# Six key tiles multiplied by VectorE straight from PSUM instead of from ScalarE's copies, in a one-core vision-tower kernel

## The chip, the core and the metric

The kernel runs on one NeuronCore of one Trainium2 chip. The metric is the device time of one execution in microseconds (us), the median of several runs. Engines are named as in the profile: PE is TensorE, DVE is VectorE, ACT is ScalarE, POOL is GpSimd, SP is SyncE, which here only issues DMAs.

## What is computed

The reference is a small vision tower on a batch of 64: a patch embedding with window attention and a class token, then a causal attention layer with residual, then a mixture of eight experts with residual. The change touches the window attention of the first stage alone. Cut to that part:

```python
pe   = conv(x, conv_w, stride 14)                   # 6x6 patches of 256 channels
grid = pe.reshape(b, C, 2, 3, 2, 3)                 # 4 windows of 3x3 = 9 positions
red  = grid.mean(axis=(3, 5))                       # one row per window
q    = _ln(red, ...) @ la_wq                        # 8 heads of 32
kv   = _ln(win, ...) @ la_wkv                       # keys and values of the 9 positions
attn = softmax(einsum('bhnd,bhnkd->bhnk', q * C**-0.5, k_), axis=-1)
agg  = einsum('bhnk,bhnkd->bhnd', attn, v_)
local_out = red + agg @ la_proj_w + la_proj_b
```

## The kernel before, in words

The rows of the first stage are (window, batch) pairs: 4 windows times 64 images are 256 rows, two window tiles of 128 partitions. Each window tile has nine positions, so there are 18 position tiles, `i` = 0 to 17; 0 to 8 belong to window tile 0, 9 to 17 to window tile 1 (`wt` in the code). Three position tiles make a group `g`, 0 to 5. The whole program is written out by hand, one instruction stream for each engine, with semaphores.

For each position tile PE makes the convolution (L429, 15 matmuls of 256 columns), ACT copies it to `pe_rows` (L802), DVE takes its mean and variance (L1195 to L1202) and POOL the reciprocal root (L1052). PE turns the group (L453), ACT and DVE split it into a high and a low part (L843, L1315), and PE multiplies it with the joined key and value weights (`keys_values`, L506, six matmuls of 512 columns for one position tile). The 512 columns of a PSUM bank are then 256 columns of keys and 256 of values. Four banks take turns: position tile `i` lands in bank 4 + i % 4. The weights are centred beforehand, so the layer norm's mean needs no subtraction and only its scale `rstd`, one number for each row and position, has to be applied.

`keys_values_copy(g)` (L863) does this on ACT: one instruction for each position tile reads all 512 columns of the bank, multiplies by `rstd` and writes keys and values to `kv_rows`; it then frees the bank (`drained[b]`), and PE may fill it with tile `i + 4`. All keys go to the same place for both window tiles, `keys`, so the copies of window tile 1 wait until the scores of tile 0 have been read (`soft_step`).

`window_scores(wt, k)` on DVE takes three positions at a time: one product of `keys` (128 partitions x 768 elements) with the query row repeated three times (L1235), then a sum over each head's 32 elements into `sc` (L1237). After three of these come the maximum and the difference (L1242, L1244), the exponential on ACT (L883), sum, reciprocal and weights `pn` (L1248 to L1252). DVE and POOL multiply the values by the weights (L355) and add thirds (L360), and PE adds up and turns the result in bank 0 (`tail_agg`, L549), which ACT copies (L874, L875) for the projection (L486). For window tile 0 POOL takes two of the thirds and both sums, and for window tile 1 one of the thirds.

Around the change the order of each engine is this. PE: key/value tiles 12 and 13, the turn of the second query row (`redT1`), tile 14, the query of window tile 1 (`q1`, L486), tiles 15, 16 and 17, `tail_agg(0)`, `tail_proj(0)`, the class token's `qkv_cls` (L626), `tail_agg(1)`. The second half of `tail_agg(1)` waits for DVE's products and its sum (L360). ACT: the two pieces of `redT1` (L806), the copies of tiles 12 to 14, the query copy (L852), a weight rounding (L889), the copies of tiles 15 to 17, the aggregate copy of window tile 0, `window_exp(1)`. DVE: `window_scores(1, 0)`, `(1, 1)`, a small copy of the class token (L1382), `(1, 2)`, `score_maximum(1)`. POOL: the products and sums of window tile 0 (L355, L360), the low part of a weight (L1142, which waits for ACT's L889), the third product of window tile 1.

Of the kernel before, what the change touches and what calls it, by code (L numbers as in the profile page):

```python
# [18 lines left out]
ACT = mybir.ActivationFunctionType  # L19
AX = mybir.AxisListType  # L20
# [6 lines left out]
C = 256  # L27
CC = C // P
NW = 9
TILES = 2 * NW  # L30
GT = 3
GROUPS = TILES // GT
HL, DL = 8, 32
# [18 lines left out]
SOFT = 11  # L52
VSTEPS = 4
REST = KCH[-1][1]
REST_PARTS = ((0, 64), (64, REST))
POOL_FROM = 3
AHEAD_A, AHEAD_B = 3, 2
TOKENS = [(1, 2), (3, 4), (0, 5)]

# [13 lines left out]
def columns(items):  # L73
    at, out = 0, {}
    for name, width in items:
# [18 lines left out]
LNS = ["conv0", "conv1", "class", "conv2", "conv3", "red0", "conv4", "conv5", "red1",  # L94
       "pool0", "pool1", "in0", "in1", "in2", "mid0", "mid1", "mid2"]
# [3 lines left out]
KV_BANKS = 4  # L99
# [19 lines left out]
def tower_kernel(nc, xa, xb, conv_w, tok_w, att_w, consts, biases, rows, ffn_w, out):  # L119
    ctx = ExitStack()  # L120
    with ctx:
        def sb(name, shape, dt=F32):
            return ctx.enter_context(nc.sbuf_tensor(name, shape, dt))

        def sem(name):
            return ctx.enter_context(nc.semaphore(name))
# [19 lines left out]
        rstd = sb("rstd", [P, len(LNS), GT])  # L146
# [3 lines left out]
        kv_rows = sb("kv_rows", [P, 3, NW, C])  # L150
        keys = kv_rows[:, 0, :, :]
        sc = sb("sc", [P, 2, NW, HL])
# [35 lines left out]
        def carve(space, *shapes):  # L188

            at, views = 0, []  # L190
            for shape in shapes:
                n = int(np.prod(shape))
                v, at = space[:, at:at + n], at + n
                names = "abcd"[:len(shape)]
                views.append(v if len(shape) == 1 else v.rearrange(f"p ({' '.join(names)}) -> p {' '.join(names)}", **dict(zip(names, shape))))
            assert at <= space.shape[1]
            return views


        red, redb, rednorm, q_rows, redsum = carve(window[:, :], *[(2, C)] * 5)  # L200
# [25 lines left out]
        inn, hb, acc, midn, ctxT, h = carve(pe_rows[:, :, :, :].rearrange("p w n c -> p (w n c)"),  # L226
                                            (RT, C), (RT, C), (RT, C), (RT, C), (2, T, B), (RT, C))
# [12 lines left out]
        bank = [ctx.enter_context(nc.psum_tensor(f"bank{i}", [P, 512], F32)) for i in range(8)]  # L240
# [28 lines left out]
        drained = [sem(f"drained{i}") for i in range(8)]  # L269
# [15 lines left out]
        rstd_done, normed_done = sem("rstd_done"), sem("normed_done")  # L285
# [6 lines left out]
        third_done = sem("third_done")  # L292
        pool_values, dve_values = sem("pool_values"), sem("dve_values")
        soft_step = sem("soft_step")
        exp_done = sem("exp_done")
        cls_step = sem("cls_step")
        gexp_done, gstep = sem("gexp_done"), sem("gstep")
# [14 lines left out]
        def wait_full(eng, b, name):  # L312

            eng.wait_ge(filled[b], FILLS[b].index(name) + 1)

        def wait_copied(eng, b, name):

            eng.wait_ge(drained[b], FILLS[b].index(name) + 1)

        def wait_split(eng, g):  # L320

            if g == 0:
                eng.wait_ge(x0_split, len(KCH))
            elif g < POOL_FROM:
                eng.wait_ge(x_split, g)
            else:
                eng.wait_ge(x_split_pool, g - POOL_FROM + 1)

# [3 lines left out]
        def spread(ap, axis, n):  # L332

            ap = ap.unsqueeze(axis)
            shape = list(ap.shape)
            shape[axis] = n
            return ap.broadcast_to(shape)
# [82 lines left out]
        def _(pe):  # L420
# [365 lines left out]
            for _, b in OUT_BANKS:  # L786
                pe.wait_ge(drained[b], len(FILLS[b]))
# [6 lines left out]
        def _(act):  # L794
# [50 lines left out]
            def two_pieces(b, name, dst, gain, shift):  # L845
                wait_full(act, b, name)
                affine(dst[:, 0, :], bank[b][:, 0:P], gain, shift, 0)
                affine(dst[:, 1, :], bank[b][:, P:2 * P], gain, shift, 1).then_inc(drained[b], 1)

            def query_copy(wt):  # L850
                wait_full(act, 3, f"q{wt}")
                act.copy(q_rows[:, wt, :], bank[3][:, 0:C]).then_inc(drained[3], 1)  # L852

            def keys_values_copy(g):
                for i in range(GT * g, GT * (g + 1)):
                    wt, n = divmod(i, NW)
                    b = 4 + i % KV_BANKS
                    wait_full(act, b, f"kv{i}")
                    if i >= NW:
                        act.wait_ge(soft_step, 2 * ((i - NW) // GT + 1))  # L860
                    k = LNS.index(f"conv{g}")
                    act.wait_ge(rstd_done, k + 1)
                    act.activation(kv_rows[:, 0:wt + 2:wt + 1, n, :], bank[b][:, :].rearrange("p (k c) -> p k c", k=2),  # L863
                                   ACT.Identity, scale=rstd[:, k, i - GT * g:i - GT * g + 1]).then_inc(drained[b], 1)

# [64 lines left out]
            window_exp(0)  # L930
            turned(5)
            two_pieces(2, "redT1", redT, "q_g", "q_b")
            keys_values_copy(4)
            query_copy(1)
            wait_full(act, CONV_BANK[TILES - 1], f"conv{TILES - 1}")
            weights_hi(0, 0, 16)
            keys_values_copy(5)
# [106 lines left out]
        def _(pool):  # L1044
# [31 lines left out]
            def patches_lo(g):  # L1076
# [5 lines left out]
                                   xs[:, g % 2, HI, 0:n].bitcast(F32), ALU.subtract).then_inc(x_lo_step, 1)  # L1082
                pool.wait_ge(x_lo_step, g - POOL_FROM + 1)
                pool.tensor_tensor(xs[0:rest, g % 2, LO, n:], x_raw[0:rest, g % RAW_X, 4, :],
# [105 lines left out]
        def _(dve):  # L1190
# [36 lines left out]
            def window_scores(wt, k):  # L1227


                ns = slice(GT * k, GT * (k + 1))  # L1230
                step = SOFT * wt + 2 * k
                for i in range(NW * wt + GT * k, NW * wt + GT * (k + 1)):
                    wait_copied(dve, 4 + i % KV_BANKS, f"kv{i}")
                wait_copied(dve, 3, f"q{wt}")
                dve.tensor_tensor(keys[:, ns, :], keys[:, ns, :], spread(q_rows[:, wt, :], 1, GT), ALU.mult).then_inc(soft_step, 1)  # L1235
                dve.wait_ge(soft_step, step + 1)
                dve.tensor_reduce(sc[:, wt, ns, :], keys[:, ns, :].rearrange("p n (h d) -> p n h d", h=HL), AX.X,  # L1237
                                  ALU.add).then_inc(soft_step, 1)

            def score_maximum(wt):  # L1240
                dve.wait_ge(soft_step, SOFT * wt + 6)
                dve.tensor_reduce(smx[:, wt, :], sc[:, wt, :, :].rearrange("p n h -> p h n"), AX.X, ALU.max).then_inc(soft_step, 1)  # L1242
                dve.wait_ge(soft_step, SOFT * wt + 7)
                dve.tensor_tensor(scs[:, wt, :, :], sc[:, wt, :, :], spread(smx[:, wt, :], 1, NW), ALU.subtract).then_inc(soft_step, 1)  # L1244
# [131 lines left out]
            dve.wait_ge(soft_step, SOFT)  # L1376
            value_product(dve, 0, 2).then_inc(third_done, 1)
            window_scores(1, 0)
            window_scores(1, 1)

            wait_full(dve, 3, "q1")
            dve.tensor_copy(hT[:, :, 0, :, :].rearrange("p c s b -> p c (s b)"), spread(tokT[:, :], 2, P)).then_inc(tok_cols, 1)  # L1382
            window_scores(1, 2)
            score_maximum(1)


# [275 lines left out]
```

## Time and profile before

| | |
|---|---|
| median of 3 runs | 234.22 us (233.64 to 235.34) |
| profiled execution | 234.87 us, its span 233.1 us |
| PE busy | 205.5 us (88% of the span) |
| DVE busy | 158.8 us (68%) |
| ACT busy | 101.4 us (44%) |
| POOL busy | 95.6 us (41%) |
| chain that ended last | PE 64%, DVE 13%, issue 9%, POOL 4%, ACT 4% |
| mean granted TensorE clock | 0.971 |

The span runs from the first to the last instruction in the trace; 1.8 us of the execution's time lie outside it. The first 130 us are the two attention stages, the rest the experts, in which PE is busy almost throughout. The chain that ended last is followed back from the last instruction, at each step to what released it. In the first stage it changes from engine to engine every few microseconds, and the places that matter for the change lie between 76 and 97 us. The granted clock is the share of TensorE's full 2.4 GHz: 1.00 is that level, 0.50 is 1.2 GHz, and a value between them is a stretch in which it changed.

### The profile page before, as it was taken

The numbers are of one execution on the slowest core, as the hardware profiler recorded it, in microseconds if no ns is written. First come the engines' busy times: TensorE is split into PE (matmuls) and PEld (weight loads), VectorE is DVE, ScalarE is ACT, GpSimd is POOL, SyncE is SP. The second block draws the span as 40 slices with busy tenths as digits, with TensorE's granted clock in tenths as the row PEclk, the third lists the DMA queues.
The fourth block names the chain that finished last, engine by engine and source line by source line (L and its number), as shares of the span: only waits on it lengthen the run. The fifth ranks groups of instructions, "written<-read, shape, count | busy, mean of one in ns | idle before, by whom it ended". The sixth has DMA issues, their size and how long they took to land.

```text
span 233.1 us, 3936 instructions
## 1 busy us (share of the span) xinstructions
PE 205.5 (88%) x1332; PEld 190.2 (82%) x1332; DVE 158.8 (68%) x357; ACT 101.4 (44%) x225; POOL 95.6 (41%) x100
## 2 busy tenths in 40 slices
PE   2989958999998973869588899999999999999984
PEld 2988938998996853747476799999999999999983
DVE  2567791586448799577987589577676776767641
ACT  3863660635334724234231157365636463626120
POOL 0054399695143963246464305333232333333200
PEclk9999997999999998899999859999999999999999
DMA  6999900008500000000000003460706071500004
GB/s 232 385 400 366 307 4 0 6 0 325 218 0 0 1 0 3 0 0 0 1 3 0 0 0 87 187 245 30 270 17 253 0 270 38 232 0 0 3 0 68
DMA packets 4890, 23.01 MB, mean 99 GB/s; under 512 B 694, under 2 KB 2444, under 8 KB 3724
## 3 DMA queue, kind: packets, MB, share of 16 engines
q1 hardware_dynamic: 3960, 21.26, 25.1%
q10 hardware_dynamic: 916, 1.58, 2.0%
q8 instruction: 8, 0.13, 0.2%
q14 instruction: 6, 0.05, 0.1%
HBM read 22.44 MB, written 0.39 MB: 98 GB/s over the span
## 4 chain that ended last, share of the span: by engine, by line
PE 64%; DVE 13%; issue 9%; POOL 4%; ACT 4%; DMA 2%; SPq 2%; ACTq 0%; DVEq 0%; POOLq 0%
PE bank L752 26%; PE bank L765 14%; PE bank L429 9%; PE bank L506 4%; PE bank L642 2%; DVE kv_rows L1235 2%; DMA raw<-xb 2%; POOL rstd L1052 2%; PE bank L549 2%; DVE stats L1195 2%; PE bank L651 1%; POOL window L1066 1%; SPq L350 1%; PE bank L453 1%; PE bank L672 1%
## 5 line engine op out<-in xcount | busy, mean ns | idle before, releaser
L752 PE MATMUL bank<-split 128*128 128x322 f32 x384 | 60.8, 320 | 0.0
L752 PEld LDWEIGHTS bank<-split 128*128 128x128 f32 x384 | 59.5, 195 | 0.0
L1180 POOL TENSOR_TENSOR split<-raw,split 128x256 fp32r<-128x256 f32 x32 | 29.0, 908 | 58.6 <-DVE split L1517 58.6
L765 PE MATMUL bank<-split 128*128 128x256 f32 x288 | 36.1, 283 | 0.6 <-DVE split L1570 0.6
L765 PEld LDWEIGHTS bank<-split 128*128 128x128 f32 x288 | 35.4, 192 | 0.8 <-DVE split L1570 0.8
L429 PE MATMUL bank<-split 128*128 128x256 f32 (+1 forms) x225 | 29.9, 294 | 0.7 <-DVE split L1294 0.7
L429 PEld LDWEIGHTS bank<-split 128*128 128x128 f32 (+1 forms) x225 | 28.8, 201 | 0.8 <-DVE split L1294 0.8
L506 PE MATMUL bank<-split 128*128 128x512 f32 x108 | 26.5, 397 | 0.0
L1019 ACT ACTIVATE vprod<-bank 128x322 f32<-128x322 f32 x32 | 14.0, 436 | 25.4 <-PE bank L752 25.3
L1564 DVE TENSOR_TENSOR vprod<-bank,vprod 128x322 f32<-128x322 f32 x32 | 15.8, 493 | 13.3 <-PE bank L752 9.3
L506 PEld LDWEIGHTS bank<-split 128*128 128x128 f32 x108 | 19.8, 188 | 3.9
L1052 POOL TENSOR_TENSOR rstd<-veps,mhalf 128x1 f32<-128x1 f32 (+2 forms) x17 | 11.4, 670 | 27.2 <-DVE veps L1202 27.0
L1027 ACT CAST split<-vprod 128x322 fp32r<-128x322 f32 x32 | 14.8, 463 | 16.7 <-DVE vprod L1564 16.6
L1512 DVE TENSOR_TENSOR split<-raw,split 128x512 fp32r<-128x512 f32 x29 | 20.1, 692 | 2.2 <-ACT split L889 2.1
L889 ACT CAST split<-raw 128x512 fp32r<-128x512 f32 x32 | 19.5, 613 | 2.4 <-DMA raw<-ffn_w 2.4
L1195 DVE BATCH_NORM_STATS2 stats<-pe_rows 128x6 f32<-128x256 f32 x24 | 9.0, 415 | 15.2 <-ACT pe_rows L802 15.0
L1556 DVE SCALAR_TENSOR_TENSOR pe_rows<-bank,wgt,pe_rows 128x256 f32<-128x256 f32 x24 | 11.2, 479 | 11.1 <-PE bank L765 11.1
L802 ACT COPY pe_rows<-bank 128x256 f32<-128x256 f32 x18 | 6.5, 374 | 24.7 <-PE bank L429 23.8
L1570 DVE TENSOR_TENSOR split<-vprod,split 128x322 fp32r<-128x322 f32 x32 | 15.9, 498 | 1.4 <-ACT split L1027 1.4
L1066 POOL TENSOR_TENSOR window<-window,pe_rows 128x256 f32<-128x256 f32 x14 | 11.7, 836 | 11.3 <-ACT pe_rows L802 10.5
L863 ACT ACTIVATE kv_rows<-bank,rstd 128x512 f32<-128x512 f32 x18 | 12.0, 690 | 6.8 <-PE bank L506 6.7
L444 PE MATMUL bank<-split 128*128 128x256 f32 (+1 forms) x45 | 7.8, 342 | 4.7 <-ACT split L816 4.7
(165 smaller groups left out, 290.9 us busy)
## 6 DMA issues: line engine op xcount, KB each, us to landing
raw<-ffn_w SPq DMA_DIRECT2D x8, 1536.0 KB, 6.5
raw<-xa SPq DMA_DIRECT2D x5, 768.0 KB
tok<-tok_w SPq DMA_DIRECT2D x1, 1536.0 KB, 11.8
tok<-tok_w SPq DMA_DIRECT2D x1, 776.0 KB, 5.9
raw<-xa ACTq DMA_DIRECT2D x1, 576.0 KB, 4.4
raw<-xb SPq DMA_DIRECT2D x6, 96.0 KB
att<-att_w SPq DMA_DIRECT2D x1, 488.0 KB, 13.2
raw<-conv_w SPq DMA_DIRECT2D x1, 384.0 KB, 5.3
```

The lines of the kernel that those rows point to most:

```text
L429: mm = pe.matmul(bank[b][:, 0:C], xs[0:n, g % 2, px, a:a + P], cws[0:n, pw, k, :], start=(k == 0 and m == 0), stop=(k == len(KCH) - 1 and ...
L506: mm = pe.matmul(bank[b][:, :], lns[:, g % 2, px, a:a + P], wkvs[:, pw, aw:aw + 2 * C], start=(c == 0 and m == 0), stop=(c == CC - 1 and m ...
L752: mm = pe.matmul(bank[b][:, 0:NCOL], aws[:, q, pw, a:a + P], ms[:, px, c, FIRST:ROWS], start=(c == 0 and m == 0), stop=(c == CC - 1 and m ...
L765: mm = pe.matmul(bank[b][:, 0:C], hids[:, px, s * FQ + q, a:a + P], bws[:, s, pw, q * C:(q + 1) * C], start=(q == 0 and m == 0), stop=(q = ...
L889: act.copy(aws[:, q, HI, :], a_raw[:, slot, q, :]).then_inc(a_hi, 1)
L1027: act.copy(hids[:, HI, s * FQ + q, FIRST:ROWS], hidf[:, q % 2, :]).then_inc(hid_hi, 1)
L1052: pool.tensor_tensor(rstd[0:parts, k, 0:n], veps[0:parts, k, 0:n], mhalf[0:parts, 0:n], ALU.pow).then_inc(rstd_done, 1)
L1066: pool.tensor_tensor(redsum[:, wt, :], pe_rows[:, wt, 0, :] if n == 1 else redsum[:, wt, :], pe_rows[:, wt, n, :], ALU.add).then_inc(sum_s ...
L1180: pool.tensor_tensor(bws[:, s, LO, q * C:(q + 1) * C], b_raw[:, s, q, :], bws[:, s, HI, q * C:(q + 1) * C].bitcast(F32), ALU.subtract).the ...
L1512: dve.tensor_tensor(aws[:, q, LO, :], a_raw[:, slot, q, :], aws[:, q, HI, :].bitcast(F32), ALU.subtract).then_inc(a_split, 1)
L1564: dve.tensor_tensor(hidf[:, q % 2, :], bank[5 + q % 2][:, 0:NCOL], sg[:, q % 2, :], ALU.mult).then_inc(hid_done, 1)
L1570: dve.tensor_tensor(hids[:, LO, s * FQ + q, FIRST:ROWS], hidf[:, q % 2, :], hids[:, HI, s * FQ + q, FIRST:ROWS].bitcast(F32), ALU.subtract ...
```

## The change

For the last six position tiles (groups 4 and 5, `i` = 12 to 17) DVE no longer reads keys that ACT has copied. `direct_scores(k)` takes the place of `window_scores(1, 1)` and `(1, 2)`: for each position one product of the bank's first 256 columns, in PSUM, with the query row; then the same sum over heads; then a new small product of the 24 sums with `rstd`, since the keys are not scaled any more. ACT copies and scales only the 256 value columns of these tiles, and waits for `keys_read`, which DVE raises after its product of the same tile. The bank is freed by ACT's copy as before. The query copy on ACT moves ahead of the copies of group 4.

```diff
+DIRECT = 4
...
+                    if g >= DIRECT:
+                        act.wait_ge(keys_read, i - GT * DIRECT + 1)
+                        act.activation(kv_rows[:, 1 + wt, n, :], bank[b][:, C:2 * C], ACT.Identity,
+                                       scale=rstd[:, k, i - GT * g:i - GT * g + 1]).then_inc(drained[b], 1)
+                        continue
...
+            query_copy(1)
             keys_values_copy(4)
-            query_copy(1)
...
+            def direct_scores(k):
+
+                g, wt = NW // GT + k, 1
+                ns = slice(GT * k, GT * (k + 1))
+                step = SOFT * wt + 2 * k
+                wait_copied(dve, 3, f"q{wt}")
+                for i in range(GT * g, GT * (g + 1)):
+                    b = 4 + i % KV_BANKS
+                    wait_full(dve, b, f"kv{i}")
+                    n = GT * k + i - GT * g
+                    ins = dve.tensor_tensor(keys[:, n, :], bank[b][:, 0:C], q_rows[:, wt, :], ALU.mult).then_inc(keys_read, 1)
+                dve.wait_ge(keys_read, GT * (g - DIRECT + 1))
+                dve.tensor_reduce(sc[:, wt, ns, :], keys[:, ns, :].rearrange("p n (h d) -> p n h d", h=HL), AX.X,
+                                  ALU.add).then_inc(soft_step, 1)
+                dve.wait_ge(soft_step, step + 1)
+                dve.wait_ge(rstd_done, LNS.index(f"conv{g}") + 1)
+                dve.tensor_tensor(sc[:, wt, ns, :], sc[:, wt, ns, :], spread(rstd[:, LNS.index(f"conv{g}"), :], 2, HL),
+                                  ALU.mult).then_inc(soft_step, 1)
...
-            window_scores(1, 1)
+            direct_scores(1)
...
-            window_scores(1, 2)
+            direct_scores(2)
             score_maximum(1)
```

On ACT, between the pieces of `redT1` and the exponential of window tile 1, the order before is this (`window` is the query row here, `filled4` means bank 4 is full, `keys_read` counts DVE's products):

```order
L806 ACTIVATE redT<-bank,tok 128x128
L863 ACTIVATE kv_rows<-bank,rstd 128x2x256 [waits rstd_done,soft_step,filled4]
L863 ACTIVATE kv_rows<-bank,rstd 128x2x256 [waits rstd_done,soft_step,filled5]
L863 ACTIVATE kv_rows<-bank,rstd 128x2x256 [waits rstd_done,soft_step,filled6]
L852 COPY window<-bank 128x256 [waits filled3]
L889 CAST split<-raw 128x512 [waits ffn_in0,filled0]
L863 ACTIVATE kv_rows<-bank,rstd 128x2x256 [waits rstd_done,soft_step,filled7]
```

and in the changed kernel (whose line numbers are a few higher):

```order
L808 ACTIVATE redT<-bank,tok 128x128
L854 COPY window<-bank 128x256 [waits filled3]
L867 ACTIVATE kv_rows<-bank,rstd 128x256 [waits rstd_done,keys_read,soft_step,filled4]
L867 ACTIVATE kv_rows<-bank,rstd 128x256 [waits rstd_done,keys_read,soft_step,filled5]
L867 ACTIVATE kv_rows<-bank,rstd 128x256 [waits rstd_done,keys_read,soft_step,filled6]
L896 CAST split<-raw 128x512 [waits ffn_in0,filled0]
L867 ACTIVATE kv_rows<-bank,rstd 128x256 [waits rstd_done,keys_read,soft_step,filled7]
```

The query copy has gone ahead of the three copies, each copy is half as wide, and each waits for `keys_read`.

On DVE, from the scores of the first third of window tile 1 to the maximum, before (`vprod` and `kv_rows` are values, keys and their products):

```order
L1235 TENSOR_TENSOR kv_rows<-kv_rows,window 128x768 [waits drained7,drained3,drained6,drained5]
L1237 TENSOR_REDUCE sc<-kv_rows 128x24 [waits soft_step]
L1235 TENSOR_TENSOR kv_rows<-kv_rows,window 128x768 [waits drained6,drained3,drained5,drained4]
L1237 TENSOR_REDUCE sc<-kv_rows 128x24 [waits soft_step]
L1382 COPY tok<-tokT 128x2x128 [waits filled3]
L1235 TENSOR_TENSOR kv_rows<-kv_rows,window 128x768 [waits drained5,drained3,drained4,drained7]
L1237 TENSOR_REDUCE sc<-kv_rows 128x24 [waits soft_step]
L1242 TENSOR_REDUCE smx<-sc 128x8 [waits soft_step]
```

and in the changed kernel, behind the first third's product, which stands as before:

```order
L1244 TENSOR_REDUCE sc<-kv_rows 128x24 [waits soft_step]
L1257 TENSOR_TENSOR kv_rows<-bank,window 128x256 [waits filled4,drained3]
L1257 TENSOR_TENSOR kv_rows<-bank,window 128x256 [waits filled5]
L1257 TENSOR_TENSOR kv_rows<-bank,window 128x256 [waits filled6]
L1259 TENSOR_REDUCE sc<-kv_rows 128x24 [waits keys_read]
L1263 TENSOR_TENSOR sc<-sc,rstd 128x24 [waits rstd_done,soft_step]
L1408 COPY tok<-tokT 128x2x128 [waits filled3]
L1257 TENSOR_TENSOR kv_rows<-bank,window 128x256 [waits filled7,drained3]
L1257 TENSOR_TENSOR kv_rows<-bank,window 128x256 [waits filled4]
L1257 TENSOR_TENSOR kv_rows<-bank,window 128x256 [waits filled5]
L1259 TENSOR_REDUCE sc<-kv_rows 128x24 [waits keys_read]
L1263 TENSOR_TENSOR sc<-sc,rstd 128x24 [waits rstd_done,soft_step]
```

Each product of 768 elements has become three of 256 that wait for a bank to be full (`filled`) and not for ACT's copy (`drained`), and each sum has a small product with `rstd` behind it. The order on PE and on POOL is the same in both kernels.

## Rows read from the trace of the kernel before

**Rows 1.** Chain that ended last, 78 to 92 us: start us, us, what
```profile
78.46 0.41 ACT window L852
...
78.99 2.47 DVE kv_rows L1235
...
82.36 1.61 DVE kv_rows L1235
...
87.12 0.29 DVE smx L1242
...
88.93 2.26 POOL vprod L355
...
91.32 4.42 PE bank L549 x24
```

**Rows 2.** Timeline, 75 to 93 us: start us, us, engine, line, operation, out<-in
```profile
75.07 3.64 POOL L355 TENSOR_TENSOR vprod<-kv_rows,pn 128x768 f32<-128x768 f32 x2 [0.93 <-DVE pn L1252]
...
77.91 4.48 PE L506 MATMUL bank<-split 128*128 128x512 f32 x18
...
78.78 4.35 POOL L360 TENSOR_TENSOR vprod<-vprod 128x768 f32<-128x768 f32 x2
...
79.69 0.69 ACT L863 ACTIVATE kv_rows<-bank,rstd 128x512 f32<-128x512 f32 x1 [0.31 <-PE bank L506]
...
82.43 0.69 ACT L863 ACTIVATE kv_rows<-bank,rstd 128x512 f32<-128x512 f32 x1 [0.67 <-PE bank L506]
...
83.28 1.58 PE L549 MATMUL bank<-con,vprod 128*128 128x128 f32 x12 [0.90 <-POOL vprod L360]
...
85.58 1.13 PE L486 MATMUL bank<-tok,aggT 128*128 128x256 f32 x4 [0.72 <-ACT aggT L875]
...
86.54 0.92 PE L626 MATMUL bank<-att,tok 128*128 128x224 f32 x4
...
92.03 0.96 DVE L360 TENSOR_TENSOR vprod<-vprod 128x768 f32<-128x768 f32 x1
```

**Rows 3.** Sources: durations in ns (minimum, median, maximum), first and last start
```profile
L1266 DVE TENSOR_TENSOR lo<-bank,window x2: 415/420/425, 92.9 to 97.6; 128x256 f32<-128x256 f32 x2
L1315 DVE TENSOR_TENSOR split<-bank,split x12: 540/548/551, 24.6 to 75.4; 128x384 fp32r<-128x384 f32 x12
L802 ACT COPY pe_rows<-bank x18: 361/373/390, 12.6 to 66.5; 128x256 f32<-128x256 f32 x18
L1361 DVE TENSOR_TENSOR gqblk<-con,gqc x1: 1552/1552/1552, 51.1 to 51.1; 128x16 f32<-128x16 f32 x1
```

**Rows 4.** Timeline of DVE, 67 to 72 us: three 256-column operations, a 768-column sum
```profile
67.05 1.08 DVE L1195 BATCH_NORM_STATS2 stats<-pe_rows 128x6 f32<-128x256 f32 x3 [5.83 <-ACT pe_rows L802]
...
70.50 0.95 DVE L1237 TENSOR_REDUCE sc<-kv_rows 128x24 f32<-128x768 f32 x1
```

**Rows 5.** Waits of PE: us in total, times, longest us
```profile
PE bank L549 <- POOL vprod L355: 3.9, 1, 3.9
PE bank L515 <- DVE split L1315: 3.5, 1, 3.5
```

**Rows 6.** Windows of one us: busy time and count by engine, granted clock, DMA share
```profile
36.00:37.00 1.00, 1.00 (x7) 1.00 (x8) 0.32 (x3) 0.00 (x0) 0.83 (x3) 0.71 0.00 0
...
91.00:92.00 1.00, 0.68 (x3) 0.71 (x4) 0.99 (x1) 0.00 (x0) 0.18 (x1) 0.52 0.00 0
...
94.00:95.00 1.00, 1.00 (x9) 1.00 (x8) 0.29 (x2) 0.00 (x0) 0.73 (x2) 0.78 0.00 0
...
132.00:133.00 1.00, 1.00 (x5) 0.74 (x4) 0.42 (x1) 0.37 (x1) 0.03 (x1) 0.50 0.00 0
...
138.00:139.00 1.00, 1.00 (x6) 1.00 (x5) 0.90 (x4) 0.09 (x1) 0.00 (x0) 0.59 0.00 0
```

**Rows 7.** Timeline of PE: 45 convolution matmuls at the full clock, and with a slow stretch
```profile
14.01 5.66 PE L429 MATMUL bank<-split 128*128 128x256 f32 x45 [0.71 <-DVE split L1294]
...
35.85 7.11 PE L429 MATMUL bank<-split 128*128 128x256 f32 x45
```

More of the change, by code:

```diff
@@ L294, in tower_kernel @@
         soft_step = sem("soft_step")
+        keys_read = sem("keys_read")
         exp_done = sem("exp_done")
```

## The prediction

> **What bounds the kernel now.** I read the page for the shares first: PE is busy most of the span, but the expert stages make up most of that. So the second view is the chain that ended last, cut to the place of the change [rows 1]. There the reader is to see that PE does not lead: the query copy on ACT (78.46) releases DVE, whose three products and sums follow one another up to the maximum at 87.12, then come the weights, POOL's product from 88.93, and PE's `tail_agg(1)` from 91.32. The first product takes 2.47 us and the second 1.61, the same work as elsewhere 0.95, because POOL's two sums run beside them from 78.78 for 4.35 us [rows 1, 2].
>
> The third view is the timeline of PE and ACT [rows 2]. The 18 matmuls of tiles 15 to 17 run without a break, 77.91 to 82.39. ACT takes tile 15 at 79.69 and tile 17 at 82.43, so two tiles take 2.74 us of PE, 1.37 each, and a reader follows its tile's last issue by 0.4 us (77.91 + 3 x 1.37 = 82.02, read at 82.43). Tile 16 needs bank 4, in which tile 12 stood. ACT had emptied it long before. This is what the change touches.
>
> The fourth view is the granted clock [rows 5, 6]. PE sat idle twice for over 3 us: 3.5 us before L515 and 3.9 us before `tail_agg(1)`. Behind each the clock fell to half: the us from 36 shows 0.71 on its way down, the us from 91 shows 0.52, and it was back in the us from 94 (0.78). One such stretch cost 45 convolution matmuls 7.11 - 5.66 = 1.45 us [rows 7].
>
> **The change part by part.** All in us of the profiled execution.
>
> Query copy first on ACT. It began at 78.46, when the last of the three wide copies was ending; PE's query matmuls were ready hardly earlier. I count 0, at most 0.1 gained. The first third's product and sum on DVE stand as before, so the next DVE product starts at 82.36 as now.
>
> The second third. One product of 1.61 goes, three of 256 columns from PSUM come. The nearest row is L1266, 0.42 each [rows 3]; three 256-column operations in a row take 1.08 in all [rows 4]. Does POOL hold them up as it did the wide product? L1315 also reads one operand from PSUM and one from SBUF, and its twelve runs stay between 540 and 551 ns, the last pair of them beside POOL's products from 75.07 [rows 2, 3]. So I take 1.08: ends at 83.44, against 83.97 before. Bounds: 1.61 if POOL holds them up after all, 1.08 if not. The sum is unchanged, 0.95 [rows 4], and the rescaling is added: its nearest row is the maximum over 72 elements, 0.29 [rows 1], taken as 0.25. Everything before the class token's copy is then 0.1 to 0.3 earlier than now, and worth nothing, since the next wait ends later.
>
> One bound of the rescaling is bad: it has two SBUF operands, and L1361, 16 elements wide, took 1.55 us where POOL was at work [rows 3]. Here the rescaling starts near 84.5, and POOL's L1142 near 84.6, since ACT's rounding now stands behind the new copies. If POOL comes first, DVE loses up to 1.3 us, and 0 to 0.7 of that reaches the last product below.
>
> The new wait, on ACT. The copy of tile 12 now needs DVE's product of tile 12: 82.36 + 0.42 = 82.78. Behind it on ACT queue the copies of tiles 13 and 14, the rounding, and the copies of tiles 15 to 17; behind its release of bank 4 waits PE with tile 16, and behind that in PE's order stand tile 17, `tail_agg(0)`, the projection and `qkv_cls`. A 256-column copy out of PSUM took 0.37 [rows 3], the 512-column one 0.69 [rows 2]; I take 0.42. Bank 4 is free at 83.25 and PE starts tile 16 at 83.3, where before it started at 77.91 + 1.37 = 79.3. PE is idle from 79.3 plus the end of its pipeline, some 3.7 to 4 us.
>
> The last product. At the full clock tile 17 can be read at 83.3 + 2 x 1.37 + 0.4 = 86.45. Then product 0.42, step 0.05, sum 0.95, step 0.05, rescaling 0.25, step 0.05: the maximum starts at 88.2, against 87.12. That is +1.1. The products of tiles 15 and 16 lie beside PE's work and cost nothing.
>
> The clock in this new hole. An idle time of 3.5 us and one of 3.9 us both brought it down [rows 5, 6]; the new one lies between the two. A low stretch that begins as PE resumes takes 1.45 from tiles 16 and 17 [rows 7]: the maximum starts at 89.7, +2.55.
>
> What is given back behind it. The chain from the maximum to the end of DVE's sum (L360, 92.03 + 0.96 = 92.99 [rows 2]) moves along unchanged. But the old hole in PE closes: `tail_agg(0)`, projection and `qkv_cls` (1.58, 1.13 and 0.92 [rows 2], with ACT's copy between them) now follow tile 17 and reach to within 2 us of `tail_agg(1)`. So I expect no low clock there. Its 24 records took 4.42; at the full clock 12 of them take 1.58 [rows 1, 2], and the second twelve start when DVE's sum is done. With +2.55: sum at 95.54, then 0.05 and 1.58, end at 97.17, against 91.32 + 4.42 = 95.74. Net +1.4. ACT's aggregate copy, which stands ahead of the exponential, is ready about when the exponential is, and is hidden.
>
> **Sum.** 0 for the query copy, +2.55 at the maximum, -1.15 at `tail_agg(1)`: +1.4, so 234.87 + 1.4 = 236.3 for an execution like the profiled one. That one lies 0.65 above the median of the runs, 234.22, so on the median I forecast 235.6. This kernel's measurement can tell about 1% (2.3 us) from no change.
>
> The Trainium skill (TensorE: Matmul & The Clock Gate, Part 1) says that the chip's watching of PE's activity is free-running and does not reset when a kernel starts. The trace agrees as far as it goes: the clock fell some 3.6 to 4 us behind the start of each idle time, not at one fixed distance. By that rule a low stretch can fall partly beside the two tiles, and the cost of 1.45 is then its upper end.
>
> **The rivals.**
>
> First, the clock stays full across the new hole. Then only +1.1 arrives at the maximum, DVE's sum ends at 94.09, and `tail_agg(1)` at 94.09 + 0.05 + 1.58 = 95.7, as now: 0.0, so 234.2 on the median. For it: the hole ends with dense matmuls. Against it: both idle times of this length brought the clock down. 25%.
>
> Second, slower by over 1%: the clock stays low twice as long. This is what the trace shows around 132 to 139 (0.50 and then 0.59 on its way up [rows 6]). There PE had short and mixed matmuls behind a gap, as it has here in `tail_agg(0)`, projection and query. Then all 2.74 of tiles 16 and 17 runs slow. At the convolutions' rate (1.45 lost in about 3.4 of slow clock) that is +2.0, the maximum +3.1, and if the clock is low again in `tail_agg(1)`, its second half takes 2.7: 96.1 + 2.7 = 98.8, +3.1 in all, 237.3 on the median. It decides once the low clock outlasts tile 17. 12%.
>
> Third, faster: PE's two low stretches near 132 are short by one, because the work arrives there at another moment. One stretch is 1.45, so with the first rival it gives 232.7. Nothing in the profile ties it to the change. 5%.
>
> That the change doesn't unhook DVE from ACT is no rival: the order shows the products waiting for `filled` alone.
>
> **How the numbers follow.** Forecast 58%, first rival 25%, second 12%, third 5%. The range goes from 233.8, a little under the first rival, to 237.4, just above the second; it leaves out the third. Slower by over 1% means above 236.6: the second rival and a few per cent of the forecast's own spread, where the rescaling is held up too: 0.15. Faster by over 1%, below 231.9: 0.05. Within 1%: 0.80.
>
> **What would show it.** In the profile after: DVE's products from PSUM at 0.42 each, the first near 82.4; the first narrow copy of ACT at 82.8; PE idle before tile 16 from about 79.7 to 83.3, released by ACT's copy; a granted clock of 0.5 in the us from 84 to 86; the maximum near 89.7; the clock at 1.0 in `tail_agg(1)`, its end near 97.2. The forecast is wrong if the clock is full at 84, if the products take over 0.6, or if PE starts tile 16 before 82.

## The result, and the profile after

The changed kernel takes 238.05 us (237.18 to 238.06, 4 runs) against 234.36 us before (233.64 to 235.34, 4 runs): ratio 1.0139, 95% interval 1.0102 to 1.0177. Two later comparisons of the same pair gave 1.0155 (1.0100 to 1.0210) and 1.0121 (1.0075 to 1.0167). Over all 16 runs of the changed kernel the median is 237.46 us, over the 87 runs of the kernel before that list a clock 234.44: 3.0 us slower, where 1.4 were forecast. The profiled execution took 238.05 us, its span 236.3. The ratios leave out the runs more than 1.5% above a kernel's fastest, and since those are the ones with the most slow clock, every count of slow stretches below, and every mean time, is over all runs instead.

The place of the change in the timeline of the changed kernel (start us, us, engine, line, operation), which answers to [rows 1, 2]:

```profile
80.28 0.37 ACT L854 COPY window<-bank 128x256 f32<-128x256 f32 x1 [1.44 <-PE bank L488]
...
80.78 2.62 DVE L1242 TENSOR_TENSOR kv_rows<-kv_rows,window 128x768 f32<-128x768 f32 x1 [1.43 <-ACT window L854]
...
84.30 1.07 DVE L1257 TENSOR_TENSOR kv_rows<-bank,window 128x256 f32<-128x256 f32 x3
84.83 1.20 ACT L867 ACTIVATE kv_rows<-bank,rstd 128x256 f32<-128x256 f32 x3 [4.18 <-DVE kv_rows L1257]
...
85.45 4.35 PE L508 MATMUL bank<-split 128*128 128x512 f32 x12 [3.82 <-ACT kv_rows L867]
...
86.40 0.18 DVE L1263 TENSOR_TENSOR sc<-sc,rstd 128x24 f32<-128x24 f32 x1
...
86.62 1.31 POOL L1149 TENSOR_TENSOR split<-raw,split 128x512 fp32r<-128x512 f32 x1 [1.56 <-ACT split L896]
...
89.84 0.42 DVE L1257 TENSOR_TENSOR kv_rows<-bank,window 128x256 f32<-128x256 f32 x1 [2.14 <-PE bank L508]
...
90.38 0.47 ACT L867 ACTIVATE kv_rows<-bank,rstd 128x256 f32<-128x256 f32 x1 [2.09 <-DVE kv_rows L1257]
...
91.51 0.28 DVE L1268 TENSOR_REDUCE smx<-sc 128x8 f32<-128x72 f32 x1
...
95.72 3.32 PE L551 MATMUL bank<-con,vprod 128*128 128x128 f32 x24 [1.74 <-POOL vprod L357]
```

The reader is to see the new chain: DVE's first direct product (84.30) releases ACT's narrow copy (84.83), that releases PE (85.45), whose 12 matmuls of tiles 16 and 17 take 4.35 us, and only then comes DVE's last product (89.84). The maximum starts 11.23 us after the query copy (91.51 - 80.28), where it was 87.12 - 78.46 = 8.66 [rows 1]. `tail_agg(1)` takes 3.32 in place of 4.42.

The longest waits of PE in it, beside [rows 5]:

```profile
PE bank L508 <- ACT kv_rows L867: 3.8, 1, 3.8
PE bank L517 <- DVE split L1341: 3.5, 1, 3.5
...
PE bank L551 <- POOL vprod L357: 1.7, 1, 1.7
```

The hole of 3.9 us before `tail_agg(1)` has shrunk to 1.7, and one of 3.8 has opened before tile 16.

The granted clock in windows of one us (the number before the last two), beside [rows 6]:

```profile
35.00:36.00 1.00, 0.00 (x0) 0.00 (x0) 0.96 (x6) 0.00 (x0) 0.86 (x2) 0.77 0.00 0
42.00:43.00 1.00, 1.00 (x9) 1.00 (x9) 0.00 (x0) 0.00 (x0) 0.92 (x2) 0.81 0.00 0
87.00:88.00 1.00, 1.00 (x4) 0.77 (x3) 0.54 (x2) 0.65 (x2) 0.93 (x1) 0.50 0.00 0
107.00:108.00 1.00, 0.81 (x2) 0.81 (x3) 0.64 (x3) 0.09 (x1) 0.76 (x2) 0.61 0.00 0
121.00:122.00 1.00, 0.55 (x3) 0.51 (x3) 0.93 (x3) 0.39 (x2) 1.00 (x3) 0.50 0.00 0
```

The clock is at half from 35.6 to 42.4, 86.8 to 90.2, 107.2 to 110.6 and 120.9 to 124.3. Before, it was so from 36.4 to 39.8, 91.0 to 94.5 and 132.0 to 138.8. The us that were spent at half clock are 17.1 here and 13.7 before, always in portions of 3.4 or twice that. I call 3.4 us at half clock a slow stretch: five here, four before.

That gave a second way to read every run, not only the profiled one. Each run lists its span and its mean granted clock, and 2 x (1 - clock) x span is the time at half clock. A line through these 103 runs of the two kernels, with one slope and two offsets, leaves a scatter of 0.5 us (standard deviation; the farthest run lies 1.4 us off): 231.1 us for the kernel before and 232.7 for the changed one, plus 0.33 us for each us at half clock, 1.1 for a stretch. The kernel before has a mean of 3.1 stretches a run (2, 3 or 4), the changed kernel 4.4 (3, 4 or 5). So the 3.0 us are two things: 1.6 that are there at an equal number of stretches, and 1.3 stretches more (plus or minus 0.4), 1.4 us. At the same number of stretches, which the forecast had assumed, the medians are 234.4 and 236.35 at three, and 235.6 and 236.7 at four: 1.9 and 1.1 apart.

### The profile page after: what moved, and what is told of

Read it like the earlier page. It is cut to its first block, busy times and chain, and to the rows that moved or that the text cites. A ratio compares the mean times of both kernels' runs of the same rounds, so it can differ in the third digit from the quotient of the medians.

```text
span 236.3 us, 3948 instructions
## 1 busy us (share of the span) xinstructions
PE 207.5 (88%) x1332; PEld 191.7 (81%) x1332; DVE 159.2 (67%) x363; ACT 100.5 (43%) x225; POOL 94.0 (40%) x100
## 4 chain that ended last, share of the span: by engine, by line
PE 66%; DVE 13%; issue 8%; ACT 4%; POOL 3%; DMA 2%; SPq 2%; ACTq 0%; DVEq 0%; POOLq 0%
PE bank L754 25%; PE bank L767 14%; PE bank L431 9%; PE bank L508 6%; DMA raw<-xb 2%; PE bank L644 2%; PE bank L628 2%; POOL rstd L1059 2%; DVE stats L1202 1%; PE bank L455 1%; PE bank L653 1%; DVE vprod L357 1%; PE bank L488 1%; POOL window L1073 1%; SPq L352 1%
## 5 line engine op out<-in xcount | busy, mean ns | idle before, releaser
L754 PE MATMUL bank<-split 128*128 128x322 f32 x384 | 59.2, 314 | 0.6 <-DVE vprod L1590 0.6
L508 PE MATMUL bank<-split 128*128 128x512 f32 x108 | 28.1, 413 | 3.8 <-ACT kv_rows L867 3.8
L431 PE MATMUL bank<-split 128*128 128x256 f32 (+1 forms) x225 | 30.8, 300 | 0.2 <-DVE split L1320 0.2
L431 PEld LDWEIGHTS bank<-split 128*128 128x128 f32 (+1 forms) x225 | 29.7, 207 | 0.3 <-DVE split L1320 0.3
L508 PEld LDWEIGHTS bank<-split 128*128 128x128 f32 x108 | 20.6, 196 | 8.3 <-issue 4.2
L1538 DVE TENSOR_TENSOR split<-raw,split 128x512 fp32r<-128x512 f32 x29 | 20.6, 712 | 2.2 <-ACT split L896 2.2
L446 PE MATMUL bank<-split 128*128 128x256 f32 (+1 forms) x45 | 8.6, 368 | 5.4 <-ACT split L818 5.4
L446 PEld LDWEIGHTS bank<-split 128*128 128x128 f32 (+1 forms) x45 | 8.1, 273 | 5.7 <-ACT split L818 5.7
```

The costliest lines, as they stand in the source:

```text
L431: mm = pe.matmul(bank[b][:, 0:C], xs[0:n, g % 2, px, a:a + P], cws[0:n, pw, k, :], start=(k == 0 and m == 0), stop=(k == len(KCH) - 1 and ...
L446: mm = pe.matmul(bank[j][:, 0:C], xs[0:n, 0, px, a:a + P], cws[0:n, pw, k, :], start=(k == 0 and m == 0), stop=(k == len(KCH) - 1 and m == 2))
L508: mm = pe.matmul(bank[b][:, :], lns[:, g % 2, px, a:a + P], wkvs[:, pw, aw:aw + 2 * C], start=(c == 0 and m == 0), stop=(c == CC - 1 and m ...
L754: mm = pe.matmul(bank[b][:, 0:NCOL], aws[:, q, pw, a:a + P], ms[:, px, c, FIRST:ROWS], start=(c == 0 and m == 0), stop=(c == CC - 1 and m ...
L1538: dve.tensor_tensor(aws[:, q, LO, :], a_raw[:, slot, q, :], aws[:, q, HI, :].bitcast(F32), ALU.subtract).then_inc(a_split, 1)
```

## The experiments

All counts of stretches below are made in this way. "At equal clock" means the offset of such a line, one slope (1.1 us a stretch) for all kernels; differences between kernels are known to about 0.5 us. This table has, for each profiled execution, the start of the second query copy on ACT, the time from it to the maximum (the part that the change touches), and from there to DVE's second `local_out` (L1266 before, L1292 in the changed kernel), which holds `tail_agg(1)`:

| kernel | query copy at | to the maximum | on to `local_out(1)` |
|---|---|---|---|
| before | 78.46 | 8.66 | 10.49 |
| before again (e1) | 79.69 | 8.67 | 10.63 |
| changed | 80.28 | 11.23 | 9.41 |
| changed again (e2) | 79.53 | 11.43 | 9.41 |
| changed, third (e8) | 78.69 | 12.23 | 10.64 |
| last group only (e3) | 81.52 | 9.14 | 10.69 |
| products early (e4) | 81.06 | 8.53 | 10.80 |
| hole filled (e5) | 79.49 | 9.89 | 10.73 |
| before, filled (e6) | 79.85 | 8.66 | 9.42 |
| early and filled (e7) | 76.91 | 8.55 | 9.42 |
| before, late tile 16 (e9) | 80.07 | 12.89 | 9.41 |
| both filled (e10) | 79.73 | 9.90 | 9.41 |
| products early, again (e11) | 80.69 | 8.56 | 10.76 |

### e1: the kernel before again, no edit

> The kernel before, unchanged, run once more as if it were a change. Of the 3.2 us between the two profiled executions, 1.9 to 2.0 us stand in the traces before the place of the change is reached (at the query copy, 78.46 against 80.28): about 0.96 from the first input transfer and about 1.0 from a slow TensorE stretch behind the wait at L515 that lasted 6.8 us and not 3.4. Theory A (this part is variation from run to run, and no effect of the change): the ratio is 1.000 within 0.5%, single times are spread over 1 to 2 us, and its profile may show another number or length of slow stretches, with a span of 231 to 236. Theory B (this part belongs to the changed program): the stretch behind L515 lasts 3.4 us again and the first transfer takes 4.7 us, as in the first profile.

Measured: ratio 1.0014 (0.9972 to 1.0055), single runs 233.25 to 236.67 us. Its profile reaches the query copy at 79.69, 1.2 us later than the first profile of the very same kernel, with slow clock for 6.8 us behind L515, where the first profile had 3.4. So what lies ahead of the change's place in the first pair of profiles is variation from run to run: theory A. The changed kernel itself reaches the query copy at 79.53 and 78.69 in e2 and e8.

### e2 and e8: the changed kernel again, no edit

> The changed kernel, unchanged, once more. Theory A: 1.2 to 2 us slower than before in the median (the +1.4 at the place of the change and little else), and the stretch behind L515 can be short in its profile. Theory B: 3 to 4 us slower again, with the long stretch behind L515 and the slow transfer back in the profile, and two slow stretches near 107 and 121 us. Both expect the hole of 3.8 us in front of tile 16 and a slow stretch behind it.

> The changed kernel once more beside the others on one chip, to count its slow stretches. Clock theory: a mean of 4 to 5 a run again, base 233.4, 237.5 to 238.3 in the median. If the count of 4.5 was chance: near 3, median 236.3 to 236.8. Its profile gives a third picture of where the stretches lie; a place that comes back each time (near 107 and near 120 us) would be an effect of the change, a place that does not is chance.

Measured: 1.0155 and 1.0121. The early slow stretch was short in both profiles, so on that point theory A held, but its 1.2 to 2 us did not: the loss stayed. Neither 107 nor 120 came back in all three (e2 has a stretch at 119 to 122.5, e8 neither), so nothing ties those places to the change. What came back each time is the hole before tile 16 and slow clock behind it. The counts are 4.5 and 4.2 stretches a run. e8's count is in the range that was expected, but its median of 236.72 is not: it lies with the other case, 236.3 to 236.8. In e8 both tiles 16 and 17 and `tail_agg(1)` were slow, as in the prediction's second rival. Its PE timeline:

```profile
83.85 5.37 PE L508 MATMUL bank<-split 128*128 128x512 f32 x12 [3.81 <-ACT kv_rows L867]
...
95.13 4.54 PE L551 MATMUL bank<-con,vprod 128*128 128x128 f32 x24 [1.97 <-POOL vprod L357]
```

and its clock:

```profile
84.00:85.00 1.00, 1.00 (x3) 0.81 (x4) 0.97 (x3) 0.94 (x3) 0.00 (x0) 0.50 0.00 0
88.00:89.00 1.00, 1.00 (x4) 0.81 (x3) 0.00 (x0) 0.00 (x0) 0.00 (x0) 0.51 0.00 0
```

Tiles 16 and 17 ran almost wholly at half clock (5.37 us for 12 matmuls, against 4.35 in the first profile and 3.0 in e5), and `tail_agg(1)` was slow again behind an idle time of only 1.97 us. From the query copy to `local_out(1)` that is 22.9 us, 3.7 more than before. The length of that idle time does not decide it: in e2 `tail_agg(1)` ran at the full clock behind the same 1.97 us:

```profile
95.16 3.32 PE L551 MATMUL bank<-con,vprod 128*128 128x128 f32 x24 [1.97 <-POOL vprod L357]
```

### e3: direct products for the last group only

```diff
-DIRECT = 4
+DIRECT = 5
...
-            direct_scores(1)
+            window_scores(1, 1)
```

> Direct products for the last three position tiles only (DIRECT = 5, window_scores(1, 1) restored). The banks of tiles 12 to 14 are then freed by ACT at once and PE has no hole in front of tile 16. If the late release of the banks is the cause: within 0.5 us of the kernel before (DVE pays three products of 1.07 for one of 0.95 and 0.2 for the rescaling: +0.3 to +0.4), no wait of PE before tile 16, the slow stretch in tail_agg(1) back. If the direct products as such cost the time (slower products, contention): about half of the loss stays, +1 us or more.

Measured: 1.0009 (0.9964 to 1.0054); over all 12 runs the mean is 0.35% above that of the kernel before (interval -0.1% to +0.8%), with 4.1 stretches a run against 2.9. No wait of PE before tile 16. DVE behind the second group:

```profile
88.34 1.07 DVE L1257 TENSOR_TENSOR kv_rows<-bank,window 128x256 f32<-128x256 f32 x3
89.45 0.95 DVE L1259 TENSOR_REDUCE sc<-kv_rows 128x24 f32<-128x768 f32 x1
90.44 0.18 DVE L1263 TENSOR_TENSOR sc<-sc,rstd 128x24 f32<-128x24 f32 x1
```

Three products take 1.07 and the rescaling 0.18 and a step, so the maximum comes 0.48 later than before, of which 0.35 is these two. The direct products as such cost that and no more: at equal clock this kernel is not above the one before (0.3 us below). For the 1.6 us it is the release of tiles 12 to 14 that matters, since only their banks have a successor that PE is about to fill. On the number of stretches this run leaves a doubt: it has no hole before tile 16, and 1.2 stretches more than the kernel before (plus or minus 1.0), two of them in its profile's `tail_agg(1)`, behind a wait of only 1.54 us:

```profile
94.87 4.60 PE L551 MATMUL bank<-con,vprod 128*128 128x128 f32 x24 [1.54 <-POOL vprod L357]
```

e4 and e11 below, with all six products direct and no hole either, have no more stretches than the kernel before.

### e4 and e11: all six direct, but the first three ahead of the wide product

`direct_scores` is cut in two, and DVE's three products of tiles 12 to 14 go first:

```diff
+            direct_products(1)
             window_scores(1, 0)
             direct_scores(1)
...
+            direct_products(2)
             direct_scores(2)
```

> The changed kernel with DVE's three direct products of tiles 12 to 14 moved ahead of window_scores(1, 0), so that ACT can free their banks before PE needs them; all else as in the changed kernel. Late-release theory: PE's wait before tile 16 falls from 3.8 us to under 0.3, the slow stretch there goes, the maximum starts within 0.6 us of the kernel before, and the time is within 0.7 us of the kernel before, 2 to 3 us under the changed kernel. Rival (the direct products or the rescaling cost it): it stays within 1 us of the changed kernel.

> The version with the early direct products, once more, since its first interval (0.982 to 0.997) was wide. From the query copy to the maximum it took 8.5 us against 8.7 before, so at equal clocks I expect no more than 0.3 us of gain: ratio 0.997 to 1.001. If the 0.9895 holds, it comes from fewer slow stretches (mean under 2.7 a run against 3.1).

Measured: 0.9895 (0.9819 to 0.9972) and 0.9949 (0.9916 to 0.9983). Over all 6 and all 12 runs the means are 0.45% and 0.38% below that of the kernel before (intervals -1.3% to +0.4%, and -0.7% to 0.0%), so the version is a little faster at best, and about 4 us under the changed kernel, more than the 2 to 3 expected. e11's ratio is below the 0.997 to 1.001 that was expected. The timeline of e4 shows why the loss is gone:

```profile
81.46 1.09 DVE L1255 TENSOR_TENSOR kv_rows<-bank,window 128x256 f32<-128x256 f32 x3 [1.35 <-ACT window L854]
...
82.46 1.71 DVE L1242 TENSOR_TENSOR kv_rows<-kv_rows,window 128x768 f32<-128x768 f32 x1
...
82.62 3.00 PE L508 MATMUL bank<-split 128*128 128x512 f32 x12 [0.21 <-ACT kv_rows L867]
...
86.06 1.09 DVE L1267 TENSOR_TENSOR sc<-sc,rstd 128x24 f32<-128x24 f32 x1
```

PE waits 0.21 us and not 3.8. The wide product, started later beside POOL's sums, takes 1.71 and not 2.5 to 2.6. The rescaling is the bad case of the prediction's bound: 1.09 us for 24 elements, because POOL's L1149 began at 85.84. The 8.53 us to the maximum are hardly less than 8.66; at equal clock this kernel lies 0.8 us under the one of before, and I can name only 0.1 of that from the traces. The rest is open. It does not come from fewer stretches, as e11's expectation had it: over all 18 runs there are 3.0 a run, as many as before.

### e5: the hole before tile 16 filled with spare matmuls

```diff
+            keys_values(GT * 5)
+            pe.wait_ge(att_in, 16)
+            for _ in range(6):
+                pe.matmul(bank[2][:, 0:C], ident, att[:, 0:C], start=True, stop=True)
+            keys_values(GT * 5 + 1)
+            keys_values(GT * 5 + 2)
-            keys_values_group(5)
```

> The changed kernel with six spare matmuls of 256 columns (about 0.5 us each, 3 us in all) on PE between tile 15 and tile 16, into a free bank: PE is busy in most of the hole, and starts tile 16 when it did before. Each run lists its mean granted clock, from which 2 x (1 - clock) x span gives the us spent at half clock; over the runs so far the time is a base of the kernel (231.7 before, 233.4 changed) plus 0.97 us for each stretch of 3.4 us at half clock, with 3.1 such stretches a run before and 4.5 changed. Clock theory (the hole brings slow stretches of its own): one to two stretches a run fewer, tiles 16 and 17 at the full clock, 1.0 to 1.9 us faster than the changed kernel. Rival (the number of slow stretches has to do with something else, such as the later stages): tiles 16 and 17 at the full clock, but the count stays above 4 and the time within 0.7 us of the changed kernel.

Measured: 1.0004 (0.9970 to 1.0039), 2.5 stretches a run. (The added wait lets the spare matmuls start only when their operand is loaded; each shows as two records in the trace.) The release of tile 16 is exactly as late as in the changed kernel; only the clock differs:

```profile
80.68 2.75 PE L616 MATMUL bank<-att,con 128*128 128x256 f32 x12
84.67 3.01 PE L508 MATMUL bank<-split 128*128 128x512 f32 x12 [1.23 <-ACT kv_rows L872]
```

Tiles 16 and 17 take 3.01 and not 4.35 or 5.37. The maximum comes 9.89 us after the query copy, 1.23 later than before, and that is what the late release costs by itself at this place. What the maximum came later still in the changed kernel (11.23, 11.43 and 12.23) was clock. Nothing was gained in this one profile behind it: `tail_agg(1)` was slow there, and `local_out(1)` comes 20.6 us after the query copy, as in the first profile of the changed kernel. The gain stands in the runs: 1.9 stretches fewer than in the changed kernel (1.7 fewer than in e8 on the same chip), at the upper end of the expected one to two, and a mean 2.0 us below e8's, where 1.0 to 1.9 were expected. At equal clock the two kernels are 0.4 us apart, which is within the error.

### e6 and e7: the old hole filled

Six spare matmuls between `qkv_cls` and `tail_agg(1)`, in the kernel before (e6) and in the version of e4 (e7):

```diff
             qkv("qkv_cls")
+            for _ in range(6):
+                pe.matmul(bank[2][:, 0:C], ident, att[:, 0:C], start=True, stop=True)
             tail_agg(1, (*range(2 * GT, NW), *range(GT)))
```

> The kernel before with the same six spare matmuls in its own hole of 3.9 us, between qkv_cls and tail_agg(1). Clock theory: tail_agg(1) takes 3.2 to 3.4 us and not 4.4, one slow stretch a run fewer (about 2), 0.9 to 1.3 us faster than before. Rival: the slow stretches only fall elsewhere, no faster than before by 0.3 us. This is also the price of what I took to be given back at tail_agg(1) by the change.

> The version with the early direct products and the six spare matmuls before tail_agg(1). If both gains add: base as e4 (230.7) and one slow stretch a run fewer, 232 to 233 in the median, 1.5 to 2 us faster than before. If they do not: at e4's time.

Measured: e6 0.9938 (0.9898 to 0.9978). Over all 12 runs the mean is 0.3% below that of the kernel before (interval -0.7% to +0.05%), with 2.3 stretches a run against 3.0 on the same chip (0.6 fewer, plus or minus 0.7). So a gain is likely, but smaller than the 0.9 to 1.3 us expected, and not shown beyond the noise. In the profile `tail_agg(1)` takes 3.32 us and starts 4.2 us after the maximum as before:

```profile
88.69 2.75 PE L681 MATMUL bank<-att,con 128*128 128x256 f32 x12
92.72 3.32 PE L549 MATMUL bank<-con,vprod 128*128 128x128 f32 x24 [1.28 <-POOL vprod L355]
```

e7 1.0015 (0.9984 to 1.0046): the median is 234.47, not the 232 to 233 of two gains that add, and over all 13 runs the mean equals that of the kernel before (234.2 against 234.3), with 2.9 stretches a run. The profiled run is the fastest of them (230.15 us, with no slow stretch in its span), 8.55 and 9.42 us in the two parts. Filling this place gave nothing here.

### e9: the kernel before with tile 16 started late

```diff
+            keys_values(GT * 5)
+            pe.wait_ge(soft_step, SOFT + 3)
+            keys_values(GT * 5 + 1)
+            keys_values(GT * 5 + 2)
-            keys_values_group(5)
```

> The kernel before with one wait added: PE starts tile 16 only when DVE's second wide product is done, some 5.5 us behind the query copy, about when the changed kernel does (5.2). No direct product, no rescaling, no other order. Late-start theory (the hole in PE is the whole cause): from the query copy to the maximum 11.4 us at the full clock and up to 12.8 with a slow stretch (8.7 before, 11.2 to 12.2 changed), 4 to 5 slow stretches a run, 2.5 to 4 us slower than before. Rival (the direct products, the narrow copies or the rescaling have a good part in it): at most 1.5 us slower than before.

Measured: 1.0167 (1.0088 to 1.0246), and 236.99 to 241.82 us over its six runs with 3 to 7 stretches, 5.4 in the mean against 3.2 before on the same chip. Over all six the mean is 2.3% above that of the kernel before (1.5% to 3.2%), 5.5 us, more than the 2.5 to 4 expected. PE waits 4.3 us:

```profile
PE bank L506 <- DVE kv_rows L1238: 4.3, 1, 4.3
```

12.89 us to the maximum, with a slow stretch on tiles 16 and 17, for which up to 12.8 was expected. Nothing of the change is in this kernel but the late start of tile 16, and it loses as much and more: 3.2 us at equal clock, and 2.2 stretches. More, because its third product has to wait for ACT's wide copy of tile 17 as well. Here `tail_agg(1)` ran at the full clock behind an idle time of 3.17 us:

```profile
97.17 3.32 PE L549 MATMUL bank<-con,vprod 128*128 128x128 f32 x24 [3.17 <-POOL vprod L355]
```

### e10: the changed kernel with both places filled

As e5, and three spare matmuls before `tail_agg(1)`:

```diff
             qkv("qkv_cls")
+            for _ in range(3):
+                pe.matmul(bank[2][:, 0:C], ident, att[:, 0:C], start=True, stop=True)
```

> The changed kernel with PE kept busy in both places: six spare matmuls before tile 16 and three more before tail_agg(1). If the count of slow stretches is made by these two places: about 2 a run (2.5 with the first place alone, 4.4 in the changed kernel), 234.3 to 235.0 in the median, with tail_agg(1) at 3.2 to 3.4 us. If not: at e5's 235.3.

Measured: 0.9988 (0.9947 to 1.0030), median 234.54 and 2.1 stretches a run, both as expected. `tail_agg(1)` at 3.32 us:

```profile
91.70 1.46 PE L688 MATMUL bank<-att,con 128*128 128x256 f32 x6
93.84 3.32 PE L551 MATMUL bank<-con,vprod 128*128 128x128 f32 x24 [0.68 <-POOL vprod L357]
```

Filling the second place took 0.4 of a stretch more off than e5 did, which is within the noise. That place is slow in some profiles (e8, e5) and not in others (the first one, e2), while the first was slow in all three profiles of the changed kernel.

## Why the prediction was wrong, point by point

- **Query copy first: 0.** Right. It starts right behind PE now, but DVE's first product starts 0.5 us after it, as before. Nothing is gained.
- **The products from PSUM, 0.42 each, 1.08 for three, not held up by POOL.** Right: 416 ns in the median of six, 412 to 425, and 1.07 for three; the first of them ran beside POOL's sum, the fourth (86.70) beside POOL's L1149. The rescaling took 0.18 in all three profiles of the changed kernel, not 0.25; it went ahead of POOL's L1149 by 0.2 us. The bad bound was real and shows in e4 (1.09).
- **The new wait.** Right: PE idle 3.8 us; ACT's narrow copy 0.47, not 0.42.
- **The late release by itself: +1.1 at the maximum.** 1.23 in e5. Over the runs the change costs 1.6 at equal clock.
- **One slow stretch on tiles 16 and 17: +2.55 in all.** +2.57 in the first profile and +2.77 in e2, but +3.57 in e8, where the clock was low for 6.8 us and so through both tiles. That also answers the sentence that took 1.45 for the upper end. The reading beside it was a little off: in the trace before, the clock fell 4.2 and 3.6 us behind the start of the two idle times. In the changed kernel it fell 5.1 us behind it, at 86.75 and not at 84, in e2 4.0 and in e8 2.1.
- **Given back at `tail_agg(1)`: -1.15.** -1.08 in the first profile and e2, which makes +1.5 and +1.7 from the query copy to `local_out(1)`, as forecast. In e8 nothing was given back, and it is +3.7.
- **The comparison of two executions.** Of the 3.2 us between the two first profiles, 1.8 lie ahead of the query copy (78.46 against 80.28), and e1 shows 1.2 of variation there in the kernel before alone. Of the first four runs of the changed kernel three had five stretches. So a part of the distance between 238.05 and the range was the draw; the median of all 16 runs, 237.46, lies at its upper end.

The step that failed is the count of slow stretches in "What is given back behind it". The sum set one stretch on tiles 16 and 17 against one taken off `tail_agg(1)` ("So I expect no low clock there") and so kept their number. The runs show 3.1 a run before and 4.4 after. The 1.3 stretches more are 1.4 us, and with the 1.6 at equal clock they make the 3.0 that came, where 1.4 had been forecast.

What shows that the new hole brings them: filling it takes 1.9 a run off the changed kernel (e5, plus or minus 0.7), making such a hole in the kernel before puts 2.2 on (e9, plus or minus 1.4), and without it the early products have as many as before (e4, e11). The stretch taken off at the old place is worth less: filling the old hole in the kernel before takes off 0.6, plus or minus 0.7 (e6), and in the changed kernel that place was slow in one profile of three. Against a clean account stands e3, with 4.1 and no hole.

The second rival named the right direction, more slow clock, and its sum of +3.1 is near the median of +3.0. That is luck in part: its pattern, both tiles slow and `tail_agg(1)` slow again, stands in e8 only, and there it cost +3.7. It got 12%, and the range ended just above it, at 237.4.

Two more points. The first rival's price of nothing is borne out by e10: with both places filled there are 2.1 stretches a run, 1.1 fewer than in the kernel before, and the mean time is the same (234.7 both). What failed is its condition, since the changed kernel does not keep the clock up by itself. And a single profiled execution was taken for the kernel: it had four stretches, one more than the median run, which is the 0.65 us that I subtracted without asking where they came from.

What stays open: where exactly the added stretches fall over many runs, since three traces of the changed kernel are few; why e3 has 4.1; and what else than 0.1 us makes e4 and e11 faster at equal clock.

## What to carry to other kernels

When an engine takes its operand straight from PSUM, the bank is held until that engine gets there; before judging the instruction's price, look for who is about to refill the bank, and put the direct reads ahead of other work of the reader. A new idle time of some 4 us on PE can cost twice: once if it is on the path, and once more through slow matmuls behind it. Do not set it off against an old one that closes without runs that count the stretches. And before reading a difference of 1% out of two traces, compare the mean granted clock of all runs; here it explained about three quarters of the variance.

## What the runs showed of the hardware

- The same kernel ran with two, three or four stretches at half clock of 3.4 us each, in 87 runs (21, 38 and 28 of them), with medians of 233.4, 234.4 and 235.6 us. That is the greater part of the scatter of 233.1 to 236.7 us; 0.45 us (standard deviation) is left beside it.
- The length of PE's idle time before `tail_agg(1)` did not decide whether it ran slow: it did behind 1.54 us (e3) and 1.97 us (e8, e5), and did not behind 1.74 (the first profile), 1.97 (e2) and 3.17 us (e9). With three spare matmuls there (1.46 us) it was at the full clock in e10. The Trainium skill (TensorE: Matmul & The Clock Gate, Part 1) says that the watching is free-running, so that the same kernel meets it at another point each time, and advises not to fit to one count; the runs agree, with 3, 4 and 5 stretches in the changed kernel (3, 4 and 9 of 16 runs). Its remark that the ramp costs under 1% of a typical kernel fits one stretch here (1.1 us of 235, 0.5%), but not the three to five of a whole run, 3.3 to 5.5 us or 1.4 to 2.3%.
- Twelve matmuls of 512 columns took 3.01 us at the full clock and 5.37 at half.
- A product of 24 elements for each partition, with both operands in SBUF, took 0.18 us alone and 1.09 beside a POOL operation (e4); L1361 took 1.55 beside two. One with an operand in PSUM took 0.42 in either case. The Trainium skill (SBUF — State Buffer, section on the two separate sides) says that a DVE operation with two SBUF inputs and a POOL operation that reads SBUF exclude each other for the whole instruction; both numbers agree with it.
